# Feed-forward, shift and attention layers in halves of 256 tokens, one group behind the recurrence, with the output projection inside the recurrence

## The reference

```python
x = x + 0.5 * gated_ffn(LN(x))        # silu(x Wg) * (x Wu), 768 hidden, Wd; int weights / 127
x = x + gated_delta_net(LN(x))        # 16 heads, keys of 64, values of 128
x = x + 0.5 * gated_ffn(LN(x))        # the same weights
x = x + 0.5 * shift_ffn(LN(x))        # mixes with the token before; sigmoid(xr Wr) * (relu(xk Wk)^2 Wv)
x = x + block_attention(LN(x))        # 16 heads of 16, rotary, causal in blocks of 64 tokens
x = x + 0.5 * shift_ffn(LN(x))        # the same weights
```

```python
S = a_t * (S - b_t * k_t (k_t^T S)) + k_t v_t ;   o_t = S^T q_t
```

## Time and profile before

| | us |
|---|---|
| median of 3 runs | 9528.12 (9527.74 to 9530.57) |
| profiled execution, its own time | 9529.48 |
| its span | 9527.7 |
| TensorE matmul busy | 7091.6 (74%) |
| VectorE busy | 4742.1 (50%) |
| GpSimd busy | 2896.9 (30%) |
| ScalarE busy | 2594.3 (27%) |
| mean granted TensorE clock | 0.846 of full speed |

### The profile page before, as it was taken

One profiled execution on the slowest core, in us unless ns is written; L12 is line 12 of the kernel. 1 busy time (PEld: TensorE's weight loads), 2 busy tenths in 40 slices (PEclk: granted clock), 3 DMA queues, 4 the chain that ended last, 5 costly groups with the idle time before them and its releaser, 6 DMA issues. The chain is left out here.

```text
span 9527.7 us, 151688 instructions
## 1 busy us (share of the span) xinstructions
PE 7091.6 (74%) x55840; PEld 4885.9 (51%) x55840; DVE 4742.1 (50%) x9325; ACT 2594.3 (27%) x5122; POOL 2896.9 (30%) x3781
## 2 busy tenths in 40 slices
PE   6777777767787777877778777787777777777777
PEld 3644546445464454645546455464554645546455
DVE  5445454454544545445454454545545455464553
ACT  2223132231322313223132231322313223132231
POOL 2315133251322513225132251322513225132251
PEclk8888888888888888888888888888888888888888
DMA  1101001010010100101001010010100101001010
GB/s 48 48 3 25 30 10 48 3 27 28 10 48 3 29 26 10 48 3 34 21 10 48 3 34 21 10 48 3 34 21 10 48 3 34 21 10 48 3 35 3
DMA packets 376009, 225.64 MB, mean 24 GB/s; under 512 B 336880, under 2 KB 353392, under 8 KB 366960
## 3 DMA queue, kind: packets, MB, share of 16 engines
q1 hardware_dynamic: 375152, 214.71, 7.5%
HBM read 155.95 MB, written 58.72 MB: 23 GB/s over the span
## 5 line engine op out<-in xcount | busy, mean ns | idle before, releaser
L538 DVE SCALAR_TENSOR_TENSOR SC<-SC,CW 128x512 f32<-128x512 f32 x1536 | 1281.9, 835 | 255.8 <-DVEq L536 170.0
L1097 PE MATMUL PS<-CST,SC 128*128 128x128 f32 x2432 | 494.7, 351 | 951.8 <-PEq L1105 520.2
L768 POOL TENSOR_TENSOR RSTD<-VAR,NHALF 128x2 f32<-128x2 f32 x192 | 133.8, 697 | 3009.0 <-POOLq L767 3009.0
L1097 PEld LDWEIGHTS PS<-CST,SC 128*128 128x128 f32 x2432 | 351.1, 177 | 1227.1 <-issue 1210.4
L839 POOL TENSOR_TENSOR WO<-WO 128x30 f32<-128x30 f32 (+14 forms) x960 | 581.9, 606 | 262.9 <-POOLq L853 126.3
L1094 PE MATMUL PS<-S,KQ 64*64 64x128 f32 x8192 | 659.2, 278 | 0.0
L842 POOL TENSOR_TENSOR WO<-WO 128x30 f32<-128x30 f32 (+14 forms) x960 | 613.8, 639 | 136.4
L1094 PE MATMUL PS<-XT,WV 128*128 128x512 f32 x1024 | 524.7, 652 | 115.0 <-PEq L1205 77.1
L862 POOL TENSOR_TENSOR FR<-MS,NHALF 128x8 f32<-128x8 f32 x128 | 210.0, 1641 | 1265.7 <-POOLq L861 1265.7
L1094 PE MATMUL PS<-XT,WQK 128*128 128x512 f32 x1024 | 576.2, 699 | 0.0
L1094 PE MATMUL PS<-WV,SC 64*64 64x128 f32 x8192 | 531.8, 280 | 41.9 <-PEq L1296 41.9
(11 more groups left out here) (159 smaller groups left out, 13423.5 us busy)
## 6 DMA issues: line engine op xcount, KB each, us to landing
WV<-in_wv SPq DMA_DIRECT2D x16, 2048.0 KB, 12.8
WO<-in_wo SPq DMA_DIRECT2D x16, 2048.0 KB, 7.5
WQK<-in_wq SPq DMA_DIRECT2D x16, 1024.0 KB, 4.8
WQK<-in_wk SPq DMA_DIRECT2D x16, 1024.0 KB, 6.9
cells_in<-SC SPq DMA_DIRECT2D x128, 128.0 KB, 2.8
WO<-cells_in SPq DMA_DIRECT2D x32, 512.0 KB, 3.3
cells_out<-WO SPq DMA_DIRECT2D x32, 512.0 KB, 2.6
cells_nat<-WO SPq DMA_DIRECT2D x32, 512.0 KB, 3.6
```

What stands on the lines that cost most here:

```text
L538: op = v.scalar_tensor_tensor(y, pre[:, j:j + G], CW[:, i * TAPS + j:i * TAPS + j + 1], y, ALU.mult, ALU.add)
L768: q.tensor_tensor(out=RSTD[:, 2 * k:2 * k + 2], in0=VAR[:, 2 * k:2 * k + 2], in1=NHALF[:, 0:2], op=ALU.pow).then_inc(rstd_ready, 1)
L1097: return nc.tensor.matmul(out_, in_, ident, is_transpose=True, start=True, stop=True)
```

## The change

`X` and `XIN` become two buffers `XS[0]` and `XS[1]`. Group n runs the stages up to the recurrence on one of them, and then the tail runs on the other one, which holds group n-1. In the first group the tail runs on zeros, and after the last group one more tail is run, so there are 17 tails for 16 groups. All the tail's stages are written as generators whose steps could be placed elsewhere; here each engine simply runs them all to the end behind its recurrence (`for _ in tail(): pass`).

```diff
+                    recurrence(p)
+                    for _ in tail(1 - p):
+                        pass
+            for _ in tail(1):
+                pass
```

**SyncE.** The load of x for the group after next goes into the buffer that the tail has just finished, behind the wait for both stores, and the q/k/v weights behind that:

```diff
+            def store(row, p):
                 for k in range(2):
                     sp.wait_ge(x_final, 1)
 ...
+                sp.wait_ge(stored, 32)
+                sp.sem_inc(stored, -32)
 ...
+            with sp.Fori(0, B * GROUPS // 2 - 1) as n:
+                for p in range(2):
+                    inverse_traffic()
+                    store(n * (2 * G) + p * G, p)
+                    load(n * (2 * G) + (p + 2) * G, p)
+                    next_qkv()
```

```diff
 # TensorE
-                        dst = cols(bank(4 + 2 * (c % 2) + x), m % 4, DV)
+                        dst = cols(bank(3 + x), m % 4, DV)
+                def projected(t):
 ...
+                    for h in range(H):
+                        i = mm(bank(2)[:, 0:D], VO[:, h * G + t * P:h * G + t * P + P], WO[:, h * D:h * D + D], h == 0, h == H - 1)
 ...
+                    i.then_inc(wo_ps, 1)
+                for c in range(CHUNKS):
+                    for x in range(2):
+                        if c >= 1:
+                            pe.wait_ge(s_ready, 1)
 ...
+                        old_state(c, x)
 ...
+                    if c >= 2:
+                        output_t(c - 2, 0)
+                    if c == 3:
+                        copied()
+                        pe.wait_ge(d_back, 96)
+                        pe.sem_inc(d_back, -96)
+                        inverse_q(1, 0, bank(2))
+                    if c == 4:
+                        copied()
+                        inverse_t(1, 1, bank(2))
+                    if c >= 1:
+                        output(c - 1, 0)
 ...
+                    solve(c, 0)
+                    solve(c, 1)
+                    if c >= 2:
 ...
+                        output_t(c - 2, 1)
+                    if c >= 1:
                         output(c - 1, 1)
 ...
+                    if c == 3:
+                        copied()
+                        inverse_q(1, 1, bank(2))
+                    if c >= 5:
+                        copied()
+                        projected(c - 5)
+                    new_state(c, 0)
+                    new_state(c, 1)
 ...
+                        if c >= 5:
+                            added()
                         keys_t(c + 1)
+                    if c == 3:
+                        pe.wait_ge(kh_ready, 1)
+                        pe.sem_inc(kh_ready, -1)
+                        inverse_t(1, 0, bank(2))
 # VectorE
+                for c in range(CHUNKS):
+                    right_side(c, 0)
+                    right_side(c, 1)
+                    if c >= 5:
+                        projected(c - 5, XS[p])
+                    s_update(c, 0)
+                    s_update(c, 1)
                     if c + 1 < CHUNKS:
                         keys(c + 1)
+                    if c >= 1:
                         mean_square(c - 1)
+                    if c >= 1:
+                        normalise(c - 1, 0)
+                        normalise(c - 1, 1)
 # GpSimd
+                for c in range(CHUNKS + 1):
+                    for k in range(2):
+                        if c < 3:
+                            substitute(1 + 10 * c + 5 * k, 6 + 10 * c + 5 * k)
+                    if c == 2:
+                        finish_cells()
+                    if c >= 1:
+                        pool.wait_ge(ms_ready, 1)
```

**The tail.** Each layer is done for 256 tokens at a time, h=0 and then h=1, and every product goes through a ring of three banks, 5 to 7 (`claim` waits until the bank's reader has freed it). Gate and up share a bank and have 256 columns. TensorE's list is:

```diff
+                transposed("x0f")
+                transposed("x1f")
+                for m in range(HT):
+                    gate_up(0, m)
+                down(0)
+                for m in range(HT):
+                    gate_up(1, m)
+                    if m == 3:
+                        transposed("x0s")
+                down(1)
+                shift(0, 0)
+                values(0, 0)
+                transposed("x1s")
+                shift(1, 0)
+                values(1, 0)
+                transposed("x0a")
+                for h in range(2):
+                    # q{h}0, q{h}1, va{h}, transposed(x1a or x0u), vd{h}0, vd{h}1, kt{h}0, kt{h}1
+                    scores(h, 0)
+                    scores(h, 1)
+                    weights_t(h, 0)
+                    weighted(h, 0)
+                    scores(h, 2)
+                    weights_t(h, 1)
+                    weighted(h, 1)
+                    scores(h, 3)
+                    weights_t(h, 2)
+                    weighted(h, 2)
+                    weights_t(h, 3)
+                    weighted(h, 3)
+                    # oa{h}, ao{h}
+                shift(0, 1)
+                values(0, 1)
+                transposed("x1u")
+                shift(1, 1)
+                values(1, 1)
```

```diff
+                    exponent(0)
+                    exponent(1)
+                    weights_t(h, 0)
+                    exponent(2)
+                    weights_t(h, 1)
+                    exponent(3)
+                    weights_t(h, 2)
+                    weights_t(h, 3)
```

In the shift layers VectorE's `mix(1, n)` (the difference and the four mixes of the second half) stands behind `values` of the first half, and `mix(0, 1)` behind the attention's last addition:

```diff
+                values(0, 0)
+                mix(1, 0)
 ...
+                    v.tensor_tensor(out=half(x, h), in0=half(x, h), in1=ps, op=ALU.add).then_inc(free, 1)
+                    dve.drain()
+                    stats(h, x)
+                    if h == 1:
+                        mix(0, 1)
```

More of the change, by code:

```diff
@@ L452, in ffn @@
[L452 to L473 removed]
+                    v.scalar_tensor_tensor(x[:, cols], bank(6 + k), 0.25 * W_SCALE ** 3, x[:, cols], ALU.mult, ALU.add)
@@ new lines, in tail @@
+                if p == 0:
+                    v.memset(PREV[:, :], 0.0)
+                stats(0, x)
+                stats(1, x)
+                yield
+                normal(0, x, TXN, txn_ready)
+                normal(1, x, TXN, txn_ready)
+                yield
+                for m in range(HT):
+                    hidden(0, m)
+                    yield
+                down(0)
+                yield
+                for m in range(HT):
+                    hidden(1, m)
+                    if m == 1:
+                        normal(0, x, TXN, txn_ready)
+                    if m == HT - 1:
+                        mix(0, 0)
+                    yield
@@ L650, in mean_square, with projected @@
                 dve.drain()
-            def recurrence():
-                keys(0)
-                for c in range(CHUNKS + 2):
-                    if c < CHUNKS:
-                        right_side(c, 0)
-                        right_side(c, 1)
-                    if c >= 2:
-                        normalise(c - 2, 0)
-                        normalise(c - 2, 1)
-                    if c < CHUNKS:
-                        s_update(c, 0)
-                        s_update(c, 1)
+            def projected(t, x):
+                dve.wait_ge(wo_ps, 1)
+                dve.sem_inc(wo_ps, -1)
+                xt = x[:, t * D:t * D + D]
+                v.tensor_tensor(out=xt, in0=xt, in1=bank(2)[:, 0:D], op=ALU.add).then_inc(wo_free, 1)
@@ L1091, in _ @@
+            for _ in tail():
+                pass
         @block.tensor
@@ new lines, in recurrence @@
+                    if c == 3:
+                        pe.wait_ge(kh_ready, 1)
+                        pe.sem_inc(kh_ready, -1)
+                        inverse_t(1, 0, bank(2))
+                added()
+                output_t(CHUNKS - 2, 0)
+                output(CHUNKS - 1, 0)
+                copied()
+                output_t(CHUNKS - 2, 1)
+                output(CHUNKS - 1, 1)
+                copied()
+                output_t(CHUNKS - 1, 0)
+                copied()
+                output_t(CHUNKS - 1, 1)
```

1277 lines of the change are left out of this document (750 added, 527 removed).

## The result

The changed kernel takes 10501.5 us (median of 4 runs, 10490.7 to 10510.1), the kernel before 9527.9 (4 runs): a ratio of 1.102, 95% interval 1.100 to 1.104. Slower, as forecast, but by 974 us instead of 617, and 52 us above the range.

A forecast was written before the change was run, and what follows sets the result against it. It took TensorE to bound the recurrence, chains of dependent steps the tail's layers, and VectorE the softmax. 16 x (22.4 + 2.7) + 15 x 2.5 + 178 = 617 us on 9529.5 gave 10146, range 9730 to 10450.

The forecast's parts named there:

- Normalise one chunk behind: Recurrence chunks: VectorE waits for FR before normalise, 3.1 us more a chunk, plus 1.2 for the clock; step 15.4 us.
- The chunk's clock term: Recurrence chunks: TensorE's new 3.9 us gap brings a lower clock, 1.2 us more a step, bounds 0 and about 7.
- The projection inside: Output-projection blocks in chunks 5 to 7 stand on the chain and hide nothing: 3 x 6.85 = 20.5 us more.
- The middle inverse: Inverse in mid-recurrence: stall, pieces and copy waits cost 12.8 us instead of 23.3, so 10.5 saved, bounds 0 to 18.
- The end: Last s_update to the projection's last addition: 30 us instead of 45.3, so 15.2 saved a group.
- The tail: Feed-forward and first shift -7.2, attention +11.7, second shift -1.8: +2.7 us a group, 178.1 us, bounds 160 to 195.
- rival A: TensorE's clock holds through the gaps, so the clock terms drop out: 9735 us; chance 15%.
- The softmax loop: Attention: ScalarE's list order closes a loop, 6.4 us a step for a half's last two steps; VectorE's own work 4.
- The boundary: Between groups VectorE waits for store and load in a row: +2.5 us, 15 times.
- Seventeenth tail: The extra tail behind the last group has no cover: 178 us, once.
- B: Half 1's matmuls cover half 0's layer norms, the tail is 54 us shorter: 8950 us, faster; chance 6%.
- C: The clock stays low in the chunks, 40 us a group: 10780 us, likelier half of that, 10450; chance 14%.

The follow-up runs named there:

- experiment 4: Changed kernel with normalise taking the previous chunk's factors, wrong for the outputs, so the wait for FR leaves the chain: 10258.6 us.
- experiment 7: Changed kernel with the three early output-projection blocks moved out of chunks 5, 6 and 7 into the end of the recurrence: 10233.6 us.
- experiment 5: Changed kernel with unread 512-column matmuls put on TensorE ahead of the tail's waits, 65 a tail: 10121.2 us.
- experiment 2: Changed kernel with the recurrence, middle inverse and output projection of the kernel before; tail, delay and seventeenth tail kept: 10000.4 us.
- experiment 6: Changed kernel with another softmax order in the lists of ScalarE, TensorE and VectorE: 10195.5 us.
- experiment 9: Kernel before's layout (own tail, old recurrence) with the tail in halves, new softmax order and 46 unread matmuls a tail: 9259.0 us, 0.971 of the kernel before.
- experiment 1: Changed kernel with each group's tail on its own tokens right behind its recurrence, and no seventeenth tail: 10216.8 us.

## Why the prediction was right or wrong

Direction and parts were right; the sizes of two, the tail and the recurrence, were not. The 357 us between 617 and 974 are 16 x 16.7 in the tail, 16 x 5.3 in the recurrence, 12 in the seventeenth tail, and -16 x 0.4 at the boundary.

- *Normalise one chunk behind*: forecast 15.4 us a step, measured 16.5. The FR wait is on the chain (experiment 4): without it the step is 13.0. The chunk's clock term was right in kind: without the wait the clock of a step is 1.00.
- *The projection inside*: forecast 20.5 on the chain, covering nothing. Measured by taking it out: 7.1 a step (experiment 7). Right.
- *The middle inverse*: 10.5 saved. The two steps around it went from 48.0 to 43.7 while an ordinary pair grew by 10.7, so 15 saved, more than forecast.
- *The end*: -15.2 forecast, -12.8 measured. The clock term of the last projection was 1.5; it is 3.0 (9.89 instead of 6.85).
- *The tail* is the step that failed, and in it the price of the clock. The sum was 178.1 us. The clock terms written out in it are 1.5, twice 2.5, 1.5 and 0.7, together 8.7 and not the 11 that rival A takes off, so without them it was 169.4. In group 8 the tail is 193.6: feed-forward with first shift, up to the first q matmul, 72.7 instead of 64.8, attention 94.1 instead of 88, second shift 26.8 instead of 25.3. Experiment 5 splits this. At a granted clock of 1.00 the three take 63.1, 84.7 and 24.6, together 172.4, where the prediction without its clock terms had 63.3, 83 and 23.1. So the chains were at most 3 us too short, and the clock, priced at 8.7, costs 21 at least; with the 2.6 us that the unread matmuls hold up it is an estimated 24, and the chains were right within 1 us. The failed sentence is the one that took the gap of 3.9 us as costly and that of 1.7 as free, from one pair of rows, and with it the softmax's small gaps. Both downs stand behind 1.92 us and I priced them at 5.1; they took 7.10. The output product of the attention (4 matmuls) stands behind 1.33 and took 3.75, against 1.97 in experiment 5. The two products of the first shift's second half (WR and WKR, 4 matmuls each) stand behind a gap of 4.58 and took 3.75 and 3.02, against 1.97 and 1.89 there: 2.9 us where I had 1.5. Nor had I asked in what state the recurrence leaves TensorE: with the old one ahead of it the next feed-forward takes 4 us less (experiment 2). What carries over is open, as the last section says.
- *Against before* the tail of group 8 grew by 18.2 us, and its three stretches by 0.7, 17.8 and -0.3: the growth sits in the attention. Before's tail had a low clock as well, 0.82, so the clock explains why the sum was too small, and the new order of the softmax why the tail is longer than before; experiment 6, which changed that order alone, gave 18 us a tail, a share of clock in it.
- *The softmax loop*: 6.4 forecast at the full clock, 6.95 and 7.3 measured at the low one, 5.7 and 6.0 at the full one (experiment 5). It is made by the order of the lists (experiment 6, which changed those of three engines at once). The loop was right, and its repair was worth more than I had expected: without it a step is 3.6 to 3.8 us.
- *The boundary*: +2.5 forecast, +2.1 measured, with the store and the load of x one behind the other. *Seventeenth tail*: as any tail, 190.2 instead of 178.

Of the rivals, A (the clock holds) is refuted by the 0.80 of the tail. Its number also took off more than the sum had in it: the written terms are 8.7 in the tail and some 9 in the recurrence, where it counts 11 and 14, and with those it would have been about 9850 and not 9735. B (the halves pay) is refuted for this order of the lists; experiment 9 is a version with halves that beats before, with help that the change does not have. C's number, 10450, is the nearest to the result, but not its place: the chunks have a clock of 0.91, higher than before, and the loss is in the end of the recurrence and in the tail. The range failed with the tail: its own bounds, 160 to 195, held the 193.7, but the forecast's range gave it only 8 us a group to either side of 178, where these bounds are 18 below and 17 above.

## What to carry over

Do not price the clock by the length of the gap ahead of a product. Take the granted clock of each stretch as a sign, and test it once by filling the waits with unread matmuls; here that alone was worth 380 us. The mean clock of a stretch is no price either, since it counts time in which TensorE had nothing to do. The seventeenth tail of after and a tail of experiment 7 have 0.78 and take 190.2 and 190.5 us; group 8's in after has 0.80 and takes 193.6:

```profile
10307.40:10497.60 190.20, 124.77 (x552) 86.71 (x552) 80.17 (x179) 31.16 (x56) 28.25 (x28) 0.78 0.01 3
5467.49:5658.00 190.51, 125.12 (x552) 87.03 (x552) 80.46 (x180) 31.07 (x56) 28.36 (x28) 0.78 0.01 2
```

When a change lays out two chains of work so that they could overlap, look in each engine's list whether they do: the same banks, buffers and delay cost 10% with the steps in a row and gave 5% with the steps interleaved, the projection moved into open waits and the softmax in its new order. Here work put into the chain's middle cost its full length, and in the waits at its end less than half of it (9.1 of 20.5, while the clock there rose from 0.74 to 0.96).

## What the runs showed of the hardware

The same product behind the same gap of 1.92 us took 7.10 us in every group of after and 5.42 in its seventeenth tail and in experiments 2 and 7; in experiment 1 it took 7.11 in 12 groups and 5.42 in 4. So the last gap does not decide the granted clock by itself. The end of the recurrence ran at 0.74 ahead of every 7.10 of after and at 0.89 or more in experiments 2 and 7, but at 0.81 ahead of 7.11 in experiment 4 and at 0.79 ahead of 5.42 in experiment 1: its mean clock does not decide it either, and what does is open. With the gaps filled the clock was 1.00 for whole tails of 172 us, and no other engine's busy time changed. Taking out a wait of 1.96 us gave 3.4 us a step, since TensorE's gap fell from 3.60 to 1.73 and the step's clock rose to 1.00.
